# Between two expert blocks, two weight pieces move behind the gated rows on ScalarE and behind the h rows on VectorE

## The reference

```python
x = x + xattn(layernorm(x), ctx)     # ctx: 8 x 1601 x 384, 16 heads, softmax(q k^T) v, @ Wo + bo
x = x + attn(layernorm(x))           # its value part has width 0: this adds zero
x = x + moe(layernorm(x))

def moe(x):                          # 8 experts, D = 512, hidden width H = 2048, top 2
    logits = x @ router_w + router_b
    gating = softmax(where(top2(logits), logits, -1e30))
    h = relu(x @ w1[e] + b1[e])      # for each expert e
    y = h @ w2[e] + b2[e]
    return sum_e gating[:, e] * y
```

## Time and profile before

| | |
|---|---|
| three runs | 1130.27, 1132.33, 1132.89 us, median 1132.33 |
| the profiled execution | 1133.02 us, its span 1131.3 us |
| busy in the span | PE 1079.0 (95%), PEld 1029.5 (91%), DVE 1002.5 (89%), ACT 728.8 (64%), POOL 503.6 (45%) |
| chain that ended last | PE 74%, DVE 12%, issue 5%, ACT 5%, DMA 2% |
| weight transfers | 76 of 1024 KB, median 5.5 us from issue to landing |

### The profile page before, as it was taken

The page is one execution under the profiler, slowest core; times in us unless marked ns, Lnnn a source line. Parts: engine busy times, 40 slices in busy tenths (PEclk is TensorE's granted clock), DMA queues, the critical chain, the costliest instruction groups (busy, mean ns, idle before and its releaser), DMA issues.

```text
span 1131.3 us, 24023 instructions
## 1 busy us (share of the span) xinstructions
PE 1079.0 (95%) x7583; PEld 1029.5 (91%) x7584; DVE 1002.5 (89%) x2273; ACT 728.8 (64%) x1506; POOL 503.6 (45%) x447
## 2 busy tenths in 40 slices
PE   5999999999999999999999999998979999899996
PEld 4889999999999999999999999986868998789885
DVE  7789989989989899999999998988979888998995
ACT  3556666656565656565666666664668777787874
POOL 5556566657556665666475655261111121221211
PEclk9999999999999999999999999999889999999998
DMA  5321221222122212112212121044787877888883
GB/s 193 105 76 45 66 64 58 58 67 63 45 56 66 66 51 71 45 46 75 66 42 80 42 66 50 2 162 150 222 261 261 280 236 230 263 274 276 248 261 105
DMA packets 86366, 138.45 MB, mean 122 GB/s; under 512 B 15816, under 2 KB 40520, under 8 KB 86336
## 3 DMA queue, kind: packets, MB, share of 16 engines
q1 hardware_dynamic: 82800, 130.07, 35.9%
q0 software_dynamic: 3536, 8.00, 3.5%
HBM read 130.88 MB, written 7.17 MB: 122 GB/s over the span
## 4 chain that ended last, share of the span: by engine, by line
PE 74%; DVE 12%; issue 5%; ACT 5%; DMA 2%; DVEq 1%; POOL 0%; SPq 0%; ACTq 0%; POOLq 0%
PE ps L427 13%; PE ps L429 12%; PE ps L428 12%; PE ps L1489 8%; PE ps L1645 8%; PE ps L1539 8%; PE ps L1520 4%; PE ps L1521 4%; PE ps L1646 3%; DVE h_mix L1327 2%; DVE w_lo L1209 1%; DVE w_lo L1217 1%; DVE h_sum L1321 1%; DMA w_raw<-in_w_dram 1%; DVE qbd_lo L1110 1%
## 5 line engine op out<-in xcount | busy, mean ns | idle before, releaser
L581 POOL TENSOR_TENSOR ctx_hi<-ctx_raw,no_query 128x1152 fp32r<-128x1152 f32 x64 | 141.9, 2217 | 266.1 <-PE ps L429 255.4
L807 ACT ACTIVATE probs<-ps,negmax 128x1152 f32<-128x1152 f32 x64 | 78.4, 1225 | 184.9 <-DVE negmax L1140 184.9
L1037 DVE SCALAR_TENSOR_TENSOR k_mix<-ps,bk_sb,k_mix 64x384 fp32r<-64x384 f32 (+1 forms) x256 | 162.2, 634 | 32.2 <-ACT k_mix L767 27.1
L427 PE MATMUL ps<-wv_hi,ctx_hi 128*128 128x256 f32 (+1 forms) x624 | 180.7, 290 | 3.8 <-DVE k_mix L1037 3.7
L585 POOL TENSOR_TENSOR ctx_lo<-ctx_raw,ctx_hi 128x1152 fp32r<-128x1152 f32 x64 | 179.9, 2810 | 5.0
L429 PE MATMUL ps<-wv_hi,ctx_lo 128*128 128x256 f32 (+1 forms) x624 | 175.1, 281 | 0.0
L428 PE MATMUL ps<-wv_lo,ctx_hi 128*128 128x256 f32 (+1 forms) x624 | 174.7, 280 | 0.0
L1645 PE MATMUL ps<-xg_mix,w_hi 128*128 128x320 f32 (+1 forms) x584 | 157.5, 342 | 14.5 <-DVE h_sum L1321 7.6
L767 ACT ACTIVATE k_mix<-ps,bk_sb 64x384 fp32r<-64x384 f32 (+1 forms) x256 | 150.9, 589 | 25.7 <-PE ps L429 21.3
L1646 PE MATMUL ps<-xg_mix,w_lo 128*128 128x160 f32 (+1 forms) x584 | 135.2, 232 | 0.0
L427 PE MATMUL ps<-ctx_hi,wk_hi 128*128 128x384 f32 (+1 forms) x384 | 133.8, 348 | 0.0
(11 more groups left out here) (233 smaller groups left out, 2633.9 us busy)
## 6 DMA issues: line engine op xcount, KB each, us to landing
w_raw<-in_w_dram SPq DMA_DIRECT2D x76, 1024.0 KB, 5.5
ctx_raw<-in_ctx_t_dram SPq DMA_DIRECT2D x48, 576.0 KB, 3.8
ctx_raw<-in_ctx_t_dram SPq DMA_DIRECT2D x16, 673.5 KB, 4.1
out_dram<-acc POOLq DMA_DIRECT2D x2, 1024.0 KB, 10.8
q_both<-q_scratch SPq DMA_DIRECT2D x14, 128.0 KB, 3.0
x<-in_x_dram SPq DMA_DIRECT2D x4, 256.0 KB, 3.5
wq_raw<-in_wq_dram SPq DMA_DIRECT2D x1, 1024.0 KB, 7.8
q_scratch<-q_out SPq DMA_DIRECT2D x1, 1024.0 KB, 7.3
```

The costliest lines, as they stand in the source:

```text
L427: pe.matmul(acc_ap, a_hi, b_hi, start=start, stop=False)
L581: nc.gpsimd.tensor_tensor(ctx_hi[slot][:, :, 0:n], ctx_raw[slot][:, :, 0:n], no_query[:].rearrange("p (o i) -> p o i", o=1).broadcast_to([ ...
L1037: last = nc.vector.scalar_tensor_tensor(out=k_mix[other, 2 * a + i, cols], in0=ps[rows, bank, 0:m], scalar=bk_sb[rows, a:a + 1], in1=k_mix ...
```

## The change

Two orders at the turn are written anew. On ACT, relu_high(0) follows low_term(0) directly, gate_rows and low_term(1) come next, and both weight pieces stand behind them, one on either side of relu_high(1). On DVE, relu_low(0) follows sum_hidden(0) directly, then comes sum_hidden(1); the two pieces stand behind it, one on either side of relu_low(1). No instruction is added or removed, and nothing inside a block is changed.

```diff
@@ ScalarE, at the turn @@
                 act.wait_ge(b1_set, b + 2)
                 low_term(b + 1, 0)
-                weight_high(b + 1, 0)
                 relu_high(b + 1, 0)
                 gate_rows(b)
                 low_term(b + 1, 1)
+                weight_high(b + 1, 0)
+                relu_high(b + 1, 1)
                 weight_high(b + 1, 1)
-                relu_high(b + 1, 1)
@@ VectorE, at the turn @@
                 take_bias(bass.ds(expert_next, 1))
                 sum_outputs(b)
-                for c in range(HIDDEN_AHEAD):
-                    sum_hidden(b + 1, c)
-                    weight_low(b + 1, c)
-                    relu_low(b + 1, c)
+                sum_hidden(b + 1, 0)
+                relu_low(b + 1, 0)
+                sum_hidden(b + 1, 1)
+                weight_low(b + 1, 0)
+                relu_low(b + 1, 1)
+                weight_low(b + 1, 1)
```

## The result

| | before | after |
|---|---|---|
| median | 1131.97 us (6 runs, 1128.62 to 1132.97) | 1139.57 us (6 runs, 1138.11 to 1142.60) |
| profiled execution, its span | 1133.02, 1131.3 us | 1138.61, 1136.9 us |
| busy PE, DVE, ACT | 95%, 89%, 64% | 95%, 88%, 64% |

The change makes the kernel slower: the ratio is 1.0074, with a 95% interval of 1.0061 to 1.0087, or some 8.4 us by the ratio; the two medians lie 7.6 us apart. The forecast was 5.5 us slower. The busy time has hardly moved (PE 1079.0 to 1077.8 us, DVE 1002.5 to 999.8, ACT 728.8 to 728.3), so what came is waiting.

A forecast was written before the change was run, and what follows sets the result against it. DVE's sum(2) at each turn was taken to bound the blocks; 4 x 1.05 narrow, 3 x 0.59 wide, 0 at turn 1 and -0.45 at turn 9 make +5.52 on 1132.33: 1137.8 us, range 1133.5 to 1140.5.

The forecast's parts named there:

- What bounds the blocks: In narrow and wide blocks DVE's sum(2) counts; what is added before it reaches the block's end in full.
- The reading of `select` in wide blocks: `select` comes after chunk 3, before DVE catches up, so PE's hidden(6) waits for sum_hidden(4) and is 0.10 us late.
- The terms of the laid-out order: sum(2) delayed by +1.05 us at narrow turns 2, 5, 6, 8 and +0.59 us at wide turns 3, 4, 7.
- The loop's edge: Between the turn's last DVE operation and sum(2): its 0.09 us taken as hidden under w_lo; otherwise the narrow term is 1.15.
- Turn 1: DVE already waits 1.99 us before sum(2) behind PE's 5.09 us gap, so 1.05 fits in: 0.
- Turn 9: No block follows; gating, then POOL's two transfers, come 0.45 us earlier: -0.45 us.
- A: Rival: PE sets the pace and h rows come earlier at turns; -3.6 us, 1128.7 us; chance 0.06.
- B: Rival: DVE's delay is made good inside the blocks, no change; 1132.3 +- 2 us; chance 0.11.
- C: Rival: PE's clock falls in longer gaps at narrow turns, up to 2.2 us at each of four; 1146.6 us; chance 0.04.
- one of the signs of being wrong: The forecast would be wrong if the clock fell below full behind any turn but the first and last.
- D: Rival: transfers land late on ACT's path in narrow blocks, up to 0.5 us eight times, +4; 1141.8 us; chance 0.05.

The follow-up runs named there:

- e6: Changed kernel with `select` moved from chunk 3 to 5, PE's row search from 4 to 6, the taking of rows from 7 to 8: 1139.92 us, ratio 1.0077.
- e3: Changed kernel with DVE's register read of the next expert's number moved from the loop's head to just ahead of `select`: 1136.51 us, ratio 1.0050.
- e1: Kernel before with the new order on ACT alone, DVE keeping the old one: 1156.13 us, ratio 1.0212.
- e2: Kernel before with the new order on DVE alone, ACT keeping the old one: 1133.32 us, ratio 1.0022.
- e8: Changed kernel with a second read of the next expert's number at the loop's head: 1147.14 us, ratio 1.0135.
- e4: Changed kernel with DVE's last two steps at the turn exchanged, w_lo(1) ahead of relu_low(1): 1141.04 us, ratio 1.0097.
- e9: Kernel before with a second read of the next expert's number at the loop's head: 1141.04 us, ratio 1.0083.

## Why the prediction was right, and where its size was off

*What bounds the blocks.* Right. DVE's sum(2) is what counts at a turn, and what is added ahead of it reaches the next turn in full: in the changed kernel sum(2) is 1.42 to 1.46 later at narrow turns and 0.98 or 0.99 at wide ones, and the distances grow by 1.40 to 1.46 and 0.99 to 1.01. The reading of `select` in wide blocks is borne out by e6.

*The terms of the laid-out order.* Right. With the read out of the edge (e3), sum(2) stands where the prediction put it to 0.03 us, and turns 2 to 9 cost +6.06 for 5.97. The terms are w_lo from under the gating, 1.05, less 0.45 at wide turns, where the gating itself comes sooner.

*The loop's edge.* This is the step that failed: "with a 1.23 us w_lo last, I take the 0.09 as hidden. If it is not, the term is 1.15." The cover was there, 1.25 us behind the branch for an edge that had taken 1.15. What the sum lacked is the read's other length, 0.80 us for 0.32, which makes the edge 1.64: 0.39 us shows at each turn, and the upper bound of 0.09 was too low as well. The two halves alone bear this out: in e1 and e2 the cover is 1.29 and 1.37 us, the read is short, and nothing shows. Seven turns at 0.35 to 0.42 are 2.7 of the missing 3.0 us; the remaining 0.3 is turn 1.

*Turn 1.* The term was 0 and came out as +0.30. The 5.1 us gap of PE stayed, as it would by the rule of the Trainium skill that the prediction cites ("Runtime: NRT & Kernel Launch", Instruction fetch mechanics). It began 1.15 us behind the mark where it had been 0.70, so it moved with the turn's work by 0.45, and sum(2) came 0.43 later. The traces have something on a fetch, too: around this gap the DMA queue named "instruction" moves 16 KB at a time, three times in the nine traces whose gap is 4.75 to 5.09 us, and twice in e3 and e8, whose gaps are 3.42 and 3.31. That fits a fetch; the queue doesn't say for which engine it fetched, so it stays unshown.

*Turn 9.* -0.41 for gating, -0.38 at the end, forecast -0.45: right.

*The rivals.* A, earlier h rows for PE: refuted; PE waits longer for DVE's sums, not shorter. B, made good in the blocks: refuted by the distances. C, the clock: seen once in the changed kernel, behind turn 5, after two waits of PE of 0.93 and 0.89 us:

```profile
985.00:986.30 1.30, 0.41 (x3) 0.42 (x4) 1.00 (x3) 0.53 (x3) 0.00 (x0) 1.00 0.91 145
986.30:990.00 3.70, 3.70 (x17) 3.32 (x16) 3.57 (x12) 2.58 (x5) 0.00 (x0) 0.54 0.94 282
```

It cost nothing there: narrow chunks are DVE's, and sum(4) follows sum(2) by 4.98 as before. But it is one of the signs of being wrong that the prediction named, and I had given it 0.04 and "little". In e4 and e6 a fall took 1.0 to 1.2 us three times and nothing once, so the danger was real, and its price there about half of the 2.2 us that I had set. D, late transfers: ACT's two waits for them are 0.9 and 0.8 us now (0.7 in two and 0.4 in one before), and no distance shows them.

*The number.* The sum was 5.5, the turns and the end give 9.00 - 0.38 = 8.6, the measured ratio 8.4 (1131.97 x 0.0074), and the medians' difference is 7.6. Against this chip's median of before the forecast would have been 1137.5; 1139.57 lies in the range. That it is only 2.1 us above is in part luck: the sum lacks 3.0 us of the distances, and the medians happen to lie 0.8 us closer together than the ratio has it.

*What stays open.* What holds up a register read that begins 2.6 to 3.0 us behind the gating; why PE's gap at the first turn is 3.4 and 3.3 us in e3 and e8 and 4.8 to 5.1 in the others; why the clock falls behind some waits and not behind others of the same length; and what makes the start of the program vary by 4.6 us over the eleven traces.

## What to carry to other kernels

Before a long operation is moved, ask what it lies beside: a w_lo that filled DVE's wait for the gating was free, and the same w_lo behind the gating costs its full length, at the end of every block whose engine has nothing in hand. A loop's edge is hidden by what stands behind the last semaphore wait of the loop's body, not by what stands in the body, and the register read in it has no fixed length: a new order can move it to where it takes 0.8 us instead of 0.3. Move the read to a place with slack before the order around it is tuned. And measure a change of 0.1 us a turn by distances between marks in the trace, where they agree to a few hundredths for turns and blocks of the same kind with the clock full, and not by spans, which differ by 3 us and more for reasons outside it.

## What the runs showed of the hardware

- DVE's sequencer holds at a semaphore wait, and branch and register read behind it run only then: the branch stands 0.12 us behind the end of the ACT instruction that releases the last wait, in the kernel before and in the changed one. From the branch to the first instruction of the next round it takes 1.15 us with a read of 0.32 and 1.64 with one of 0.80 (with two reads, 2.27 in e8 and 2.47 in e9, turn 5).
- A register read on DVE from a table is 0.30 to 0.34 us or 0.79 to 1.00 us; all the long ones begin 2.61 to 2.95 us behind the end of ACT's gating, where the first packets of POOL's scatter begin (2.59 to 2.65).
- PE's granted clock fell from 1.00 to 0.54 after two waits of 0.93 and 0.89 us (the changed kernel, turn 5), and to 0.63 after one of 1.80 (e4, turn 6); each is a mixture of the two levels, 2.4 and 1.2 GHz, over the stretch read. Matmuls of 128x256 that take 0.33 us take 0.52 to 0.53 at the low level. The Trainium skill ("TensorE: Matmul & The Clock Gate", Part 1) has the throttled clock as the default that activity releases; these rows agree, but the same wait of 1.80 us left the clock full at turn 2 of e4.
